# Reordering the crossing from attention to feed-forward in a linear-attention layer, and the moves of one gated row and one x load in the feed-forward

## The reference

```
h = layernorm(x) * (1 + ca) + sa
q, k, v = split(h @ W_qkv + b_qkv)          # 8192 x 1536
q = elu(q * 32**-0.5) + 1.0001;  k = elu(k) + 1.0001
out[t] = (q[t] . sum_{s<=t} k[s] v[s]^T) / (q[t] . sum_{s<=t} k[s] + 1e-6)     # per head
x = x + ga * (out @ W_out + b_out)
h = layernorm(x) * (1 + cb) + sb
x = x + gb * ((silu(h @ wg.T) * (h @ wu.T)) @ wd.T)     # wg, wu: 1536 x 512, wd: 512 x 1536
```

## Time and profile before

| | |
|---|---|
| median of 3 runs | 2108.07 us (2107.64 to 2109.33) |
| the profiled execution | 2109.39 us, of which the span is 2107.6 us |
| TensorE busy | 2055.4 us, 98% |
| VectorE busy | 1581.5 us, 75% |
| ScalarE busy | 1006.0 us, 48% |
| GpSimd busy | 991.0 us, 47% |
| mean DMA rate over the span | 131 GB/s |
| attention | from 0 to about 1086 us |
| feed-forward | from about 1086 us to the end |

### The profile page before, as it was taken

The page is one execution under the profiler, slowest core; times in us unless marked ns, Lnnn a source line. Parts: engine busy times, 40 slices in busy tenths (PEclk is TensorE's granted clock), DMA queues, the critical chain, the costliest instruction groups (busy, mean ns, idle before and its releaser), DMA issues. The chain is left out here.

```text
span 2107.6 us, 41310 instructions
## 1 busy us (share of the span) xinstructions
PE 2055.4 (98%) x14832; PEld 1669.0 (79%) x14832; DVE 1581.5 (75%) x2152; ACT 1006.0 (48%) x1733; POOL 991.0 (47%) x790
## 2 busy tenths in 40 slices
PE   5999999999999999999989999999999999999999
PEld 4788888888888888888868878788887888878787
DVE  7988988989989889889785674757557575674744
ACT  5444454455544555444434643535455354643533
POOL 2635545555454465544454344444434444344444
PEclk9999999999999999999999999999999999999999
DMA  7011122221232222222156465554656546465543
GB/s 254 31 52 58 65 86 86 96 91 56 78 99 81 91 68 79 86 81 80 65 171 229 153 220 170 193 181 145 209 179 199 179 153 211 153 219 170 168 157 109
DMA packets 157150, 276.60 MB, mean 131 GB/s; under 512 B 11105, under 2 KB 35681, under 8 KB 157026
## 3 DMA queue, kind: packets, MB, share of 16 engines
q1 hardware_dynamic: 156498, 273.73, 39.4%
q10 hardware_dynamic: 528, 1.05, 0.1%
HBM read 208.67 MB, written 66.06 MB: 130 GB/s over the span
## 5 line engine op out<-in xcount | busy, mean ns | idle before, releaser
L1429 POOL TENSOR_TENSOR h_lo<-y_rows,h_hi 128x512 fp32r<-128x512 f32 x192 | 246.7, 1304 | 406.9 <-ACT h_hi L1530 406.9
L424 POOL TENSOR_TENSOR x_res<-y,x_res 128x512 f32<-128x512 f32 x64 | 82.2, 1284 | 302.0 <-DVE y L843 302.0
L820 DVE RECIPROCAL r_den<-r_den 128x512 f32<-128x512 f32 x64 | 213.7, 3340 | 0.0
L582 ACT ACTIVATE z_exp<-pj,qk_neg 128x512 f32<-128x512 f32 x128 | 88.2, 689 | 213.9 <-PE pj L1073 186.6
L1073 PE MATMUL pj<-xt_hi,w_hi 128*128 128x512 f32 x512 | 151.0, 416 | 8.7 <-ACT xt_hi L574 4.2
L825 DVE TENSOR_TENSOR probs<-sc,causal 128x512 f32<-128x512 f32 x256 | 158.3, 678 | 1.3 <-PE sc L1101 1.3
L1836 PE MATMUL sc<-wd,h_hi 128*128 128x512 f32 x384 | 151.9, 396 | 5.7 <-DVE y L1666 5.7
L1836 PE MATMUL sc<-wd,h_lo 128*128 128x512 f32 x384 | 149.7, 390 | 0.0
L1642 DVE TENSOR_TENSOR r_den<-pj,k_tok 128x512 f32<-128x512 f32 x96 | 66.2, 689 | 103.5 <-ACT k_tok L1513 54.6
L1073 PE MATMUL pj<-xt_lo,w_hi 128*128 128x512 f32 x512 | 140.2, 396 | 0.9 <-DVE xt_lo L792 0.9
L1073 PE MATMUL pj<-xt_hi,w_lo 128*128 128x512 f32 x512 | 138.3, 392 | 0.0
(11 more groups left out here) (252 smaller groups left out, 5643.9 us busy)
## 6 DMA issues: line engine op xcount, KB each, us to landing
w_hi<-parts SPq DMA_DIRECT2D x48, 1024.0 KB, 5.2
w_lo<-parts SPq DMA_DIRECT2D x48, 1024.0 KB, 5.2
x_mid<-x_res SPq DMA_DIRECT2D x96, 256.0 KB, 2.1
x_res<-in_L_attn_x SPq DMA_DIRECT2D x64, 256.0 KB, 3.0
xg<-in_L_attn_x SPq DMA_DIRECT2D x15, 1024.0 KB, 6.9
x_res<-x_mid SPq DMA_DIRECT2D x60, 256.0 KB, 3.8
full<-x_mid SPq DMA_DIRECT2D x60, 256.0 KB, 3.3
parts<-r_den SPq DMA_DIRECT2D x48, 256.0 KB, 2.3
```

Source lines behind the costliest of these rows:

```text
L424: pool.tensor_tensor(out=x_res[:, slot, :], in0=y[:, :], in1=x_res[:, slot, :], op=ALU.add).then_inc(y_ready, 1)
L582: act.activation(z_exp[:, n % 2, :], pj[:, n % 2, :], ACT.Relu, bias=qk_neg[:, 1 - kind, c:c + 1], scale=-scale).then_inc(below_ready, 1)
L820: dve.reciprocal(r_den[parity][:, c, :], r_den[parity][:, c, :]).then_inc(rden_ready, 1)
L1429: pool.tensor_tensor(out=h_lo[b], in0=h[i], in1=h_hi[b].bitcast(F32), op=ALU.subtract).then_inc(h_lo_ready, 1)
```

## The change

In the last group of attention the low halves `a_lo` are made by VectorE instead of GpSimd. All four of its tiles are concerned. The low halves of T3 and T4 for the first group of the feed-forward move from GpSimd to VectorE too. The order on TensorE, VectorE and ScalarE there is written anew: two transposes stand ahead of the numerators, the sums T1 and T2 stand before the division, p1 of block 1 stands ahead of the last output projection, and one reciprocal moves from the last group into the one before. GpSimd does the last two residuals of attention only after both low halves of T3 are there. On SP the weight blocks for q = 3 are issued ahead of the gb row. In every group of the feed-forward but the last the second gated row of the second half stands two instructions earlier on VectorE. The x load of group G+2 stands after the third store of the second half of group G, where `load_x(G + 1)` stood at the start of group G; group 0 still loads group 1's at its start. The diff, cut to its core:

```diff
@@ gpsimd, attention
-            a_low(g * GT)
+            if not last:
+                a_low(g * GT)
...
-            last_residual(g, 3)
-            a_low(g * GT + 3)
+            if not last:
+                last_residual(g, 3)
+                a_low(g * GT + 3)
...
+        def last_tiles():
+            last_residual(NG - 1, 3)
             residual(NG * GT - 1, 1)
@@ scalar, attention, last group
-                for op in (B22, T1, T2, T4):
+                for op in (T1, B22, T2):
                     high(0, op, 0)
-                evacuate(NG + 1, 2, sc[:, 3, :])
+                evacuate(NG + 1, 2, sc[:, 1, :])
+                evacuate(NG + 1, 3, sc[:, 3, :])
+                high(0, T1, 1)
+                high(0, B22, 1)
             a_high(g * GT + 3)
...
@@ vector, attention
+        def a_low(tile):
+            dve.wait_ge(a_hi_ready, tile + 1)
+            dve.tensor_tensor(out=a_lo[:, :], in0=a_t[:, :], in1=a_hi[:, :].bitcast(F32),
+                              op=ALU.subtract).then_inc(a_lo_ready, 1)
...
-            recip(g, parity, 3)
             if ahead:
                 feature(n, other, 0)
+            if not last:
+                recip(g, parity, 3)
+            if last:
+                norm_stats(NG + 1, range(2))
             gate_last(g, 0)
             divide(g * GT, g, parity, 0)
+            if last:
+                norm_stats(NG + 1, range(2, 3))
+                a_low(g * GT)
+                norm_stats(NG + 1, range(3, GT))
+                norm_var(NG + 1)
...
+            if last:
+                norm_x(NG + 1, range(1))
+                a_low(g * GT + 1)
+                norm_x(NG + 1, range(1, GT))
...
             gate_last(g, 2)
+            if last:
+                sum_of(0, T1, 0)
             divide(g * GT + 2, g, parity, 2)
+            if last:
+                sum_of(0, T2, 0)
+                a_low(g * GT + 2)
...
@@ tensor, attention
-            wait(pe, y_gated, tile - 1)
+            wait(pe, y_gated, min(tile - 1, (NG - 1) * GT - 1) if isinstance(tile, int) else tile - 1)
...
@@ k_turn
                 pe.wait_ge(v_ready, NG * C)
+                pe.wait_ge(a_ready, tile)
...
             if not ahead and t >= 2:
-                pe.wait_ge(probs_ready, (tile + 1) * HPC)
-                turn_second(2 * t - 4, sc[:, 3, :])
+                for i in range(2):
+                    pe.wait_ge(probs_ready, tile * HPC + 2 * i + 2)
+                    turn_second(2 * t - 4 + i, sc[:, 2 * i + 1, :])
             numerators(tile, g, parity, t)
-            if not ahead and t >= 2:
-                turn_second(2 * t - 3, sc[:, 1, :])
@@ sync, feed-forward
-            if not last:
-                load_x(G + 1)
+            if isinstance(G, int) and G == 0:
+                load_x(1)
...
+                    if i == FT + 2 and (not isinstance(G, int) or G + 2 < FG):
+                        load_x(G + 2)
...
         def groups_after():
+            sp.wait_ge(att.op_ready, NG * GT)
+            load_parts(0, 3)
             sp.wait_ge(att.y_gated, NG * GT)
             sp.dma_start(gb_row[:, :], gb_dram.broadcast_to([P, D])).then_inc(gb_in, 16)
-            sp.wait_ge(att.op_ready, NG * GT)
-            load_parts(0, 3)
@@ gpsimd, feed-forward
-            for k in range(2):
-                low(0, T4, k)
-            last_tile()
-            for k in range(2):
-                low(0, T3, k)
+            pool.wait_ge(b_ready[T3], 2)
+            last_tiles()
@@ scalar, feed-forward
             save_p1(0, 0)
-            save_p5(0, 0)
+            high(0, T2, 1)
             silu1(0, 0)
             act.wait_ge(att.op_ready, NG * GT)
             high(0, T3, 0)
             high(0, T3, 1)
+            save_p5(0, 0)
+            high(0, T4, 0)
+            high(0, T4, 1)
@@ vector, feed-forward, body
             sum_of(G + 1, T3, 1)
+            gate_y(G, FT + 1)
             sum_of(G + 1, T4, 1)
             low(G + 1, B11, 1)
-            gate_y(G, FT + 1)
             low(G + 1, B21, 1)
+            gate_y(G, FT + 2)
             low(G + 1, T1, 1)
-            gate_y(G, FT + 2)
...
@@ vector, groups_after
             add_c11(0, 0)
+            low(0, T1, 1)
+            sum_of(0, T4, 0)
+            sum_of(0, T4, 1)
+            low(0, T2, 0)
+            low(0, T2, 1)
+            sum_of(0, T3, 1)
+            low(0, B22, 0)
+            low(0, B22, 1)
+            low(0, T3, 0)
+            low(0, T3, 1)
+            add_c12(0, 0)
+            low(0, T4, 0)
+            low(0, T4, 1)
             last_tile()
...
@@ tensor, feed-forward
         p1(0, 0)
         p2(0, 0)
+        p1(0, 1)
         last_projection()
         p5(0, 0)
```

85 lines of the change are left out of this document (49 added, 36 removed).

## The result

The changed kernel takes 2101.39 us, median of 6 runs (2097.96 to 2103.08); the kernel before, on the same chip, 2108.17 us (2106.52 to 2109.33). The ratio is 0.9965, 95% interval 0.9955 to 0.9975: 6.8 us or 0.35% faster. Forecast were 2101 us and a gain of 0.34%. The profiled execution took 2100.71 us, its span is 2099.0 us (before: 2109.39 and 2107.6).

What follows compares the result with a forecast made beforehand. It took TensorE's idle time and low clock in the crossing, some 15 us, and 7 us of waits as the bound. 2109.4 - 4.3 - 1.0 - 2.0 = 2102.1 us, as a median say 2101, range 2095 to 2106.

Steps and rivals of the forecast that it cites:

- The frame: Crossing: 8 to 10 us look gained by p5, but transfers behind the last attention store give most back.
- The gated row, -4.3: Seven feed-forward turns: second gate earlier, third gate late next; 0.6 of 0.97 us kept per turn, -4.3 us.
- The x load, -1.0: Six turns: earlier load ends VectorE's 12.1 us of waits, of which TensorE felt two, so -1.0 us.
- Its price on SP: Turns: x load's issues and 2 MB ahead of later stores and residual loads cost 0, up to 1 us a turn.
- rival C: Turns: x load amid the stores delays the last residual and hidden low halves, 2119 us; chance 0.05.
- The crossing up to the last projection, -3.3: Attention tiles 61 to 63: faster low halves on VectorE start the last projection at 1086.1 instead of 1089.42, -3.3 us.
- What is given back: Behind tile 63's late gate: VectorE waits 7 us for gb, TensorE 5.5, clock falls, x decides a block later.
- The chain from the last projection to the residual: Tile 63: projection, ScalarE work, `add_c12`, low halves and gate make some 9.2 us, residual at about 1095.3.
- The ring order: SP queue behind the last store: 1 MB of weights issued first delays the gb row by 2.6 us.
- The crossing's term, -2.0: Attention to feed-forward: p5 of block 3 at 1115.8 instead of 1117.8, -2.0 us, bounds -4.8 and +2.
- Rival B: Turns and crossing: third gate takes over the wait, crossing only breaks even, 2105 us; chance 0.17.
- Rival A: Crossing: keeps the 8 to 10 us it frees, 2094 us; chance 0.14.

Runs made afterwards that it cites:

- experiment 5: Changed kernel with the three clamps of group 0, first to need the gb row, at blocks 3 to 5 instead of 1 to 3: 2102.64 us.
- experiment 6: Changed kernel with the three clamps of group 0 at blocks 3 to 5 and the statistics of group 1's x later too: 2099.68 us.
- experiment 9: Changed kernel with the gb row issued ahead of the 1 MB of weights for block 3 on SP: 2099.77 us.
- experiment 10: Changed kernel with late clamps and group 1 statistics, SP issuing gb row, weights of blocks 3 to 5, then x and residual rows: 2095.15 us.
- experiment 12: Kernel before, old crossing, with both turn edits, late clamps and statistics, and SP's gb row and weights ahead of x: 2101.31 us.
- experiment 3: Changed kernel with the second and third gated rows back at their old places on VectorE: 2105.11 us.
- experiment 2: Changed kernel with the x load put back at the start of the group: 2107.0 us.
- experiment 4: Changed kernel with both the gates and the x load at the turns put back, so the new crossing alone: 2107.7 us.
- experiment 7: Changed kernel with GpSimd's four low halves of B11 and B21 ahead of tile 60's last residual: 2097.85 us.
- experiment 1: Kernel before with only the two edits at the turns, earlier gates and the x load after the third store: 2100.65 us.

## Why the prediction was right, and which of its terms were not

The time was right, to 0.4 us. Two of its three terms were off, to opposite sides, so that it came so close is in part luck. The frame held: transfers behind the last store eat the crossing's gain (experiments 5, 6, 9, 10 and 12).

- **The gated row, -4.3.** By the rows 0.82 became 0.39 (the forecast said: third gate late next, TensorE waits 0.5 us at row FT+6), 0.43 each. Experiment 3 gives 3.7 us for it with x there, 0.53 a turn, and the marks 0.59. Right in mechanism and near in size. But the prediction's own figures give 0.97 - 0.5 = 0.47 a turn and -3.3, not the 0.6 and -4.3 that it wrote; the size is nearer to what was measured than the working was. What the prediction did not see is that it holds only with x there: experiment 2 against 4 gives 0.7.
- **The x load, -1.0.** Mis-sized. The step that failed: "TensorE felt two of those, 1.0 us". VectorE's waits were 12.1 us, and only two of TensorE's were put down to `add_c12`; but by the marks a turn got 1.16 us shorter, of which the gate explains 0.5 to 0.6. What is left, about 0.6 us in every turn and 3.6 in all, goes to x's wait, most of it without an entry in TensorE's list. The load alone measured 2.6 us (4 against 3), and 5.6 with the gates moved (2 against the changed kernel). Its price on SP was put at 0: the longer waits of GpSimd, 57.3 against 33.7 us, were there, and VectorE and TensorE have no wait for the low halves behind them. Right, and rival C is out.
- **The crossing up to the last projection, -3.3.** This step failed: 1089.19 instead of 1086.1, only -0.2. The prediction took 0.96 us for each norm of tile 61, the mean of a row of four, at whose start GpSimd stood idle for 0.8 us. Beside GpSimd's four low halves, one behind the other, the three behind the first took 1.44 each, and `a_lo` 1.75 instead of 0.60, so the masks of tile 62 came at 1072.85, 2.6 us later than before. The clock fell at 1069 to 1073 too, but TensorE still waited 0.83 us for the masks at 1074.18, so it was the masks that decided. Experiment 7 moves just these low halves away: counted from the turn of k of tile 60, the third projection comes 1.75 us earlier, the last one 2.1 and the first turn 2.3. Another 0.63 us of the 3.1 is the late turn of k of tile 60, behind the moved reciprocal, which the prediction left out; no run moves it back.
- **What is given back.** Right in mechanism: gate 63 behind `add_c12`, VectorE before the gb row (forecast 7 us, measured 6.16), TensorE behind it (5.5; 3.96), a clock at the low level for 5 us (the same; from p5 of block 2 to p5 of block 3 it took 8.83 us, forecast 8.9), x due a block later. The chain from the last projection to the residual was right too, 8.9 us where 9.2 were forecast, but it starts at 1089.19: the residual comes at 1098.06, not at 1095.3, and the store 0.7 us earlier than before, not 3.4. The ring order was over-rated. The prediction let 1 MB of weights delay the row by 2.6 us; experiment 9 shows 0.9. By the Trainium skill, "DMA: Bandwidth & Descriptors", section "Queues, rings and completion order", descriptors of one ring are taken in order; the run agrees in sign, with 0.9 us. As forecast, the sum didn't hang on it, since x decided a block later (experiments 5 and 9).
- **The crossing's term, -2.0,** measured -0.8 by the marks, -0.6 in experiment 4, and +0.7 between experiment 1 and the changed kernel, all within what repeated runs differ by. p5 of block 3 came at 1117.44, forecast 1115.8, before 1117.95 (the prediction has 1117.8).

Sum: -4.3 - 1.0 - 2.0 = -7.3 was forecast; the marks say about -4.2 (gates, 0.57 six times and 0.8 at the turn without an x load), -3.6 (x) and -0.8 (crossing) = -8.6. This division gives the gates what they bring with x there; the table of experiments 1 to 4 shows that another order of the two would divide it otherwise. An error of -2.6 for x and one of +1.2 for the crossing partly cancelled. The rest of the closeness came from the executions: the prediction took 1.3 us off since the profiled one before lay above its median, and the profiled one after lay 0.7 below its own. Rival B (2105) had the crossing nearly right, which broke even, and the gates wrong: the wait at row FT+6 was 0.39 us and not 0.8. Rival A gave 8 to 10 us for a crossing that keeps what it frees. It came near the right amount (6.2, and 9.1 with experiment 7) for a kernel that this change was not yet: it needed another order of the transfers.

## What to carry to other kernels

A wait that is taken away uncovers the next transfer in the queue, here three in a row (the gb row, x, the weights of block 4). Taking away the first gave nothing, the second 1.7 us and the third 4.5 more. So list all consumers behind a common store with their times of need, and issue in that order. What moves the store itself is not eaten in this way, since all that stands behind it moves along (experiment 7, 3.5 us). Two edits on one chain can't be priced apart: with the new crossing the gates gave 0.7 us alone and 3.7 with x there. And a wait in the list of one engine can cost another more than its own list shows: measure the distance of a mark that recurs once per turn, and divide.

## What the runs showed of the hardware that was not expected

- **VectorE beside GpSimd.** GpSimd's low half starts at 1065.44, the norm on VectorE at 1065.52 and takes 1.48 us, the subtraction behind it 1.75. In experiment 7, with GpSimd's instructions earlier, the norm starts 0.4 us before the end of GpSimd's third and takes 0.66, and the last norm, with GpSimd idle, takes 0.54. GpSimd's third low half there, and in the kernel before the four masks of tile 62 with GpSimd's low halves beside them:

```profile
1064.24 1.27 POOL L1455 TENSOR_TENSOR xt_hi<-full,w_hi 128x512 fp32r<-128x512 f32 x1
```
```profile
1070.24 2.47 DVE L825 TENSOR_TENSOR probs<-sc,causal 128x512 f32<-128x512 f32 x4
```
```profile
1068.56 5.37 POOL L1419 TENSOR_TENSOR xt_hi<-full,w_hi 128x512 fp32r<-128x512 f32 x4
```

The Trainium skill, "SBUF — State Buffer", says in "SBUF: two separate sides" that the two share a port pair, that GpSimd contends for it with VectorE's instructions of two SBUF inputs or in a two-port mode, and that whoever starts first holds it for its whole instruction. The rows agree: the norm ends 0.3 us behind the end of the GpSimd instruction that it met, at 1067.00 behind 1066.71 and in experiment 7 at 1065.80 behind 1065.51, whenever it began; the subtraction ends 0.55 behind. The masks, which read the scores from PSUM, are not slowed: 0.60 us from start to start beside GpSimd.
- **The row spread over 128 partitions was a slow load.** `ga_row<-gb_dram`, 256 KB, landed 5.5 us after its issue before, 6.6 behind weights and 5.7 at the head of the queue. While it runs the DMA engines are busy and move little; the kernel of experiment 9:

```profile
1098.00:1100.00 2.00, 1.95 (x9) 1.29 (x9) 0.08 (x1) 1.82 (x4) 0.59 (x1) 1.00 0.95 115
...
1102.00:1104.00 2.00, 0.00 (x0) 0.00 (x0) 1.19 (x3) 0.00 (x0) 0.00 (x0) 1.00 1.04 399
```

A share of 0.95 moves 115 GB/s with the row, and 1.04 moves 399 with weights and x. The weights behind it then landed 7.8 us after their issue, against 5.8 when ahead of it. So its place in the queue moves the cost and doesn't remove it. Why it is slow no run here shows.
